# Attention in three bf16 parts instead of two float32r parts, one core

## The reference

```python
def attention(x):                       # x is layernorm(input)
    q, k, v = x @ Wq.T + bq, x @ Wk.T + bk, x @ Wv.T + bv
    q, k = rope(heads(q, 16)), rope(heads(k, 4))
    att = einsum('bhgqd,bhkd->bhgqk', q, k) / sqrt(16)
    att = softmax(where(causal, att, -inf))
    return join(einsum('bhgqk,bhkd->bhgqd', att, v)) @ Wo.T + bo

x = x + attention(layernorm(x))
h = layernorm(x)
topv, topi = top_k(h @ gate_w.T, 8);  w = softmax(topv)
x = x + sum_over_chosen(w * (silu(h @ gate) * (h @ up)) @ down) + shared(h)
```

## Time and profile before

| | us |
|---|---|
| median of 3 runs | 1209.62 (1207.33 to 1210.61) |
| the profiled execution's own time | 1211.74 |
| its span, first to last instruction | 1209.9 |

### The profile page before, as it was taken

The page is one execution under the profiler, slowest core; times in us unless marked ns, Lnnn a source line. Parts: engine busy times, 40 slices in busy tenths (PEclk is TensorE's granted clock), DMA queues, the critical chain, the costliest instruction groups (busy, mean ns, idle before and its releaser), DMA issues. The chain is left out here.

```text
span 1209.9 us, 23638 instructions
## 1 busy us (share of the span) xinstructions
PE 1031.7 (85%) x7305; PEld 812.9 (67%) x7305; DVE 705.3 (58%) x2197; ACT 662.3 (55%) x1586; POOL 717.5 (59%) x953
## 2 busy tenths in 40 slices
PE   3699888898989888989998710899989999999985
PEld 1466666666666666656665400899979999989973
DVE  2476676767676767676675370222226666666676
ACT  1466665665565656655654300566656666666651
POOL 3111122774764747747557777377777777777772
PEclk9799999999998999999998855799999999999996
DMA  2388786821321312303222794777769999998755
GB/s 94 130 258 293 237 268 208 278 101 37 108 75 57 111 44 96 114 16 101 79 95 97 275 309 164 214 217 220 219 217 335 343 337 326 366 321 305 250 196 200
DMA packets 142825, 233.20 MB, mean 193 GB/s; under 512 B 17303, under 2 KB 119910, under 8 KB 137840
## 3 DMA queue, kind: packets, MB, share of 16 engines
q1 hardware_dynamic: 67936, 101.06, 25.9%
q0 software_dynamic: 27600, 69.28, 15.9%
q10 hardware_dynamic: 47168, 61.35, 15.4%
HBM read 107.32 MB, written 132.53 MB: 198 GB/s over the span
## 5 line engine op out<-in xcount | busy, mean ns | idle before, releaser
L1495 POOL DMA_INDIRECT res_d<-y,dst_i x319 | 316.7, 993 | 114.6 <-issue 83.4
L463 POOL DMA_INDIRECT rows_d<-pay,slot_i x256 | 256.5, 1002 | 73.4 <-issue 68.4
L868 DVE TENSOR_REDUCE nmax<-ps 128x1 f32<-128x512 f32 (+3 forms) x448 | 225.7, 530 | 103.7 <-PE ps L518 101.4
L736 ACT ACTIVATE wgu_s<-ps 128x512 f32<-128x512 f32 x320 | 191.7, 600 | 95.1 <-PE ps L518 91.5
L1414 PE MATMUL psB<-wgu_s,xT 128*128 x1276 | 172.2, 279 | 4.9 <-ACT innerT L1306 4.1
L518 PE MATMUL ps<-mask,ident_b 128*128 128x256 bf16 (+1 forms) x640 | 173.3, 271 | 0.0
L511 PE MATMUL ps<-kT,qT 96*128 96x512 f32 (+3 forms) x512 | 167.4, 389 | 6.7 <-DVE nmax L868 4.2
L1431 PE MATMUL psD<-wdp_s,innerT 128*128 x638 | 166.9, 385 | 0.0
L558 PE MATMUL ps<-qT,kT 128*128 128x512 f32 (+3 forms) x512 | 162.8, 380 | 0.8 <-ACT qT L749 0.6
L1414 PEld LDWEIGHTS psB<-wgu_s,xT 128*128 128x128 f32 x1276 | 157.9, 195 | 6.1 <-issue 5.8
L1217 DVE TENSOR_TENSOR inner<-inner,psB 128x128 f32<-128x128 f32 x160 | 45.7, 286 | 194.9 <-ACT inner L1302 189.8
(11 more groups left out here) (264 smaller groups left out, 1579.5 us busy)
## 6 DMA issues: line engine op xcount, KB each, us to landing
rows_d<-blank ACTq DMA_DIRECT2D x8, 5440.0 KB, 19.5
xg<-rows_d SPq DMA_DIRECT2D x160, 272.0 KB
yk<-res_d SPq DMA_DIRECT2D x28, 1024.0 KB
wgu_s<-wgu_in ACTq DMA_DIRECT2D x8, 1024.0 KB, 14.4
x_d<-x SPq DMA_DIRECT2D x30, 192.5 KB, 2.7
xs<-x_d SPq DMA_DIRECT2D x30, 192.5 KB, 2.8
res_d<-y,dst_i POOLq DMA_INDIRECT x319
wgu_s<-x_in SPq DMA_DIRECT2D x32, 128.0 KB, 2.1
```

Source lines behind the costliest of these rows:

```text
L463: pool.indirect_dma_start(rows_d, bass.IndirectOffsetOnAxis(ap=slot_i[par][:, t, k:k + 1], axis=0), pay[par][:, t, :], None).then_inc(s_sc ...
L736: act.activation(pexp[p % 4][:, s, :], ps2[:, (5 * p + s) % 2, :], ACT.Exp, scale=HEAD_D ** -0.5).then_inc(s_exp, 1)
L868: return dve.tensor_reduce(nmax[u][:, tile, heads[0]:heads[-1] + 1], src, AX.X, ALU.max, negate=True)
L1495: pool.indirect_dma_start(res_d, bass.IndirectOffsetOnAxis(ap=dst_i[:, j % (2 * G):j % (2 * G) + 1], axis=0), y[:, j % Y, :], None, bounds ...
```

## The change

Queries, keys and maxima are split into three bf16 parts (high, middle, low). A score is one matmul over 96 rows of a single head, six products of parts: the query rows are (high, high, high, middle, middle, low) and the key rows (low, high, middle, high, middle, high), 16 rows each. Each key head is stored once instead of twice. A tile has 16 transposes for its queries and 4 for its keys, in bf16 (8 and 8 in float32r before), copied by ScalarE in two copies of 1024 columns and one of 512 (four of 512 before). The maxima have 8 transposes (4 before) and one copy of 1024 columns (512 before). VectorE splits the queries in three steps and the maxima in four operations (two before). GpSimd splits the keys, at k 8 of `pre`, in four operations; VectorE did so before. Semaphores that count these steps change with them. Ones for the maxima's rows of `kT` are filled in by VectorE once at the start instead of being part of each tile's keys. Between the phases, a wait between two VectorE steps is taken out.

```diff
-            qT = two("qT", [P, PAIRS_OF_HEADS, SEQ], F32R)
-            kT = two("kT", [P, 2 * KV_HEADS, SEQ], F32R)
+            qT = two("qT", [P, HEADS, SEQ], BF16)
+            kT = two("kT", [P, KV_HEADS, SEQ], BF16)
+            mt = two("mt", [P, 2, TILES, P], BF16)
+            qs = two("qs", [P, HEADS, 8, HEAD_D], BF16)
+            ks = two("ks", [P, KV_HEADS, 8, HEAD_D], BF16)
...
+                    if k == 8:                                   # GpSimd, pre
+                        pool.wait_ge(s_hi, tile + 1)
+                        kr = rope[u][:].rearrange("p n a d -> p (n a d)")[:, D:QK_D].rearrange("p (g d) -> p g d", d=HEAD_D)
+                        pool.tensor_tensor(kr, kr, ks[u][:, :, 1, :], ALU.subtract).then_inc(s_kstep, 1)
+                        pool.wait_ge(s_kstep, 3 * tile + 1)
+                        for part in (2, 4):
+                            last = pool.tensor_copy(ks[u][:, :, part, :], kr)
+                        last.then_inc(s_kstep, 1)
+                        pool.wait_ge(s_kstep, 3 * tile + 2)
+                        pool.tensor_tensor(ks[u][:, :, 0, :], kr, ks[u][:, :, 2, :], ALU.subtract).then_inc(s_kstep, 1)
...
+                    if k == 9:                                   # TensorE, pre
+                        pe.wait_ge(s_lo, tile + 1)
                         for half in range(2):
-                            if k == 10:
-                                pe.wait_ge(s_split, 4 * tile + half + 1)
-                            for n in range(4):
-                                last = pe.transpose(psp[:, half, n * P:(n + 1) * P].bitcast(F32R),
-                                                    src[:, 2 * half + n // 2, n % 2].rearrange("p c d -> p (c d)"), ident_r[:])
+                            for n in range(8):
+                                last = pe.transpose(psp[:, half, :].bitcast(BF16)[:, n * P:(n + 1) * P],
+                                                    qs[u][:, 8 * half + n].rearrange("p c d -> p (c d)"), ident_b[:])
                             last.then_inc(s_split_ps, 1)
+                    if k == 10:
+                        pe.wait_ge(s_kstep, 3 * (tile + 1))
+                        pe.wait_ge(s_split, 3 * tile + 1)
+                        for n in range(KV_HEADS):
+                            last = pe.transpose(psp[:, 0, :].bitcast(BF16)[:, n * P:(n + 1) * P],
+                                                ks[u][:, n].rearrange("p c d -> p (c d)"), ident_b[:])
+                        last.then_inc(s_split_ps, 1)
...
-                    pe.matmul(ps1[:, bank, at:at + keys], qT[par][0:96, p, i * P:(i + 1) * P],
-                              kT[par][0:96, 2 * (p // 2) + ab, 0:keys], start=(at == 0), stop=False,
+                    pe.matmul(ps1[:, bank, at:at + keys], qT[par][0:96, 2 * p + ab, i * P:(i + 1) * P],
+                              kT[par][0:96, p // 2, 0:keys], start=(at == 0), stop=False,
...
-                    for i in range(TILES):                       # TensorE, max_up
-                        last = pe.transpose(ps1[:, 1, i * P:(i + 1) * P].bitcast(F32R), mt[p % 2][:, i, :], ident_r[:])
+                    for n in range(2 * TILES):
+                        last = pe.transpose(ps1[:, 1, :].bitcast(BF16)[:, n * P:(n + 1) * P],
+                                            mt[p % 2][:, n // TILES, n % TILES, :], ident_b[:])
...
-                        act.copy(qs[u][:, :, 0:2, :], flat[:, 0:D].rearrange("p (n d) -> p n d", d=32).unsqueeze(2)
-                                 .to_broadcast([P, PAIRS_OF_HEADS, 2, 32]))
-                        kh = flat[:, D:QK_D].rearrange("p (g d) -> p g d", d=HEAD_D)
-                        for part in (0, 2):
-                            last = act.copy(both_places(part), kh.unsqueeze(2).to_broadcast([P, KV_HEADS, 2, HEAD_D]))
-                        last.then_inc(s_hi, 1)
+                        act.copy(qs[u][:, :, 0:3, :], flat[:, 0:D].rearrange("p (n d) -> p n d", d=HEAD_D).unsqueeze(2)
+                                 .to_broadcast([P, HEADS, 3, HEAD_D]))
+                        act.copy(ks[u][:, :, 1:6:2, :], flat[:, D:QK_D].rearrange("p (g d) -> p g d", d=HEAD_D).unsqueeze(2)
+                                 .to_broadcast([P, KV_HEADS, 3, HEAD_D])).then_inc(s_hi, 1)
...
-                        act.copy(qT[par][96:128, p, :], ps1[96:128, 1, :].bitcast(F32R)).then_inc(s_m, 1)
+                        act.copy(qT[par][96:P, 2 * p:2 * p + 2, :],
+                                 ps1[96:P, 1, :].bitcast(BF16).rearrange("p (a n) -> p a n", a=2)).then_inc(s_m, 1)
...
+                for k in range(2):                               # VectorE, at the start
+                    dve.memset(kT[k][96:P], 1.0)
...
-                        dve.tensor_tensor(qs[u][:, :, 2, :], flat[:, 0:D].rearrange("p (n d) -> p n d", d=32),
-                                          qs[u][:, :, 0, :], ALU.subtract)
-                        kf = flat[:, D:QK_D].rearrange("p (g d) -> p g d", d=HEAD_D)
-                        dve.tensor_tensor(both_places(1), kf.unsqueeze(2).to_broadcast([P, KV_HEADS, 2, HEAD_D]),
-                                          both_places(0), ALU.subtract).then_inc(s_lo, 1)
+                        qr = flat[:, 0:D].rearrange("p (n d) -> p n d", d=HEAD_D)
+                        dve.tensor_tensor(qr, qr, qs[u][:, :, 0, :], ALU.subtract).then_inc(s_qstep, 1)
+                        dve.wait_ge(s_qstep, 2 * tile + 1)
+                        dve.tensor_copy(qs[u][:, :, 3:5, :], qr.unsqueeze(2).to_broadcast([P, HEADS, 2, HEAD_D])
+                                        ).then_inc(s_qstep, 1)
+                        dve.wait_ge(s_qstep, 2 * (tile + 1))
+                        dve.tensor_tensor(qs[u][:, :, 5, :], qr, qs[u][:, :, 3, :], ALU.subtract).then_inc(s_lo, 1)
...
-                        dve.tensor_copy(mt[u][:, :, 96:98], nmax[u][:]).then_inc(s_mhi, 1)
-                        dve.wait_ge(s_mhi, U + 1)
-                        dve.tensor_tensor(mt[u][:, :, 98:100], nmax[u][:], mt[u][:, :, 96:98],
+                        largest_of = nmax[u][:].rearrange("p t a -> p a t")
+                        dve.tensor_copy(mt[u][:, :, :, 96], largest_of).then_inc(s_mhi, 1)
+                        dve.wait_ge(s_mhi, 2 * U + 1)
+                        dve.tensor_tensor(nrest[u][:], largest_of, mt[u][:, :, :, 96], ALU.subtract)
+                        dve.tensor_tensor(mt[u][:, :, :, 97], largest_of, mt[u][:, :, :, 96],
+                                          ALU.subtract).then_inc(s_mhi, 1)
+                        dve.wait_ge(s_mhi, 2 * (U + 1))
+                        dve.tensor_tensor(mt[u][:, :, :, 98], nrest[u][:], mt[u][:, :, :, 97],
                                           ALU.subtract).then_inc(s_msplit, 1)
```

More of the change, by code:

```diff
@@ L135, in build @@
             nmax = two("nmax", [P, TILES, 2], F32)
+            nrest = two("nrest", [P, 2, TILES], F32)
             oT = two("oT", [P, KV_HEADS, SEQ], F32)
@@ L172, in build @@
              s_esum, s_erec, s_rw, s_cnt_ps, s_cnt, s_new, s_base_ps, s_base, s_diag, s_rank_ps, s_thd, s_pl,
[L173 removed]
+             s_slot, s_sloti, s_tk, s_pool, s_mhi, s_var1, s_var2, s_qstep, s_kstep) = [sem(n) for n in (
                  "const_in memsets consts_converted stats1 moments1 rstd1_ready xn_ready xnT_psum xnT_ready "
@@ L180, in build @@
                  "base_ready diag_ready rank_psum rows_read place_chain slots_ready slot_ints taken_step "
-                 "pool_chain max_hi var1_ready var2_ready").split()]
+                 "pool_chain max_step var1_ready var2_ready q_split_step k_split_step").split()]
             s_late = sem("later_consts_in")
@@ L217, in ending @@
                 return isinstance(h, int) and h * 2 + par >= BATCH - n
-            def both_places(part):
-                two = ks_flat[:].rearrange("p g (a e) -> p g a e", a=2)
-                return two[:, :, :, 32 * part:32 * part + HEAD_D]
             def x2_at(h, par, t):
@@ L408, in attention_pool @@
                     pool.memset(v1[k][:, :, :, 16:17], 1.0)
-                pool.memset(row0[0:1, :], 1.0)
-                for ab in range(2):
-                    pool.memset(ks[:, :, ab, 3, ab:ab + 1].bitcast(F32), 1.0)
-                    last = pool.memset(ks[:, :, ab, 3, ab + 2:ab + 3].bitcast(F32), 1.0)
-                last.then_inc(s_memset, 1)
+                pool.memset(row0[0:1, :], 1.0).then_inc(s_memset, 1)
                 pool.wait_ge(s_const, 32)
@@ L481, in pre @@
                         pe.wait_ge(s_xn, tile + 1)
-                        pe.wait_ge(s_split, held(4 * (tile - ago + 1) - 1))
+                        pe.wait_ge(s_split, held(3 * (tile - ago + 1)))
                         for c in range(KC):
@@ L487, in pre @@
                         pe.wait_ge(s_xnT, tile + 1)
-                        pe.wait_ge(s_split, held(4 * (tile - ago + 1)))
                         for c in range(KC):
@@ L717, in pre @@
```

(22 more changed lines are left out.)

36 lines of the change are left out of this document (11 added, 25 removed).

## The result

The changed kernel took 1279.2 us (median of 4 runs, 1267.7 to 1284.2) beside 1210.1 for the kernel before (1207.3 to 1212.7): ratio 1.0554, 95% interval 1.0502 to 1.0606. I had said 1222, in a range of 1199 to 1237. The direction was right, the size was not: +67 us by the ratio (+69 by the two medians) instead of +12. The profiled execution is the quickest of the four (1267.7 us, span 1265.9), so its trace shows 56 us of it.

A forecast was written before the change was run, and what follows sets the result against it. The bound was taken to change hands between TensorE and VectorE, with GpSimd third in scatter batches. Terms summed to +13 on the profiled 1211.74, so 1225; less 2.1 for the median, 1222.6, said as 1222, range 1199 to 1237.

The forecast's parts named there:

- TensorE, scores and transposes: Attention phase: bf16 scores save 35 us, query transposes 9, maxima transposes add 6; TensorE's own time -38 us (-29 to -67).
- The weight load: TensorE's score weights: 0.20 us in f32, 0.10 in bf16; were both equal, scores save about nothing and the sum ends at 1236.
- VectorE's share: Query and maxima splits in batches 2 to 6: 5.7 us a batch added, 59% and again 60% counted, +2.0.
- The 60%: Share of TensorE's gain and VectorE's additions counted outside GpSimd's stretch, TensorE being the bound a little over half the time.
- at 60% and was hardly waited for: ScalarE's wider copies: at most +0.43 us a unit and +0.3 a tile, costed at nothing except in the first tiles.
- GpSimd, +1.8 a batch: Key split in the stretch 456 to 489 us: adds 3.0, less 1.2 us of GpSimd idling, in batches 2 to 6.
- Start, +1.5: First tiles: query split +0.85 and some 1 us of wider copies, less the shorter key part, +1.5 us.
- Batch 7, the expert phase: Last batch, with no next batch to prepare: -0.5 us; expert phase after it: unchanged.
- the forecast's sum of +13: Whole kernel: batches 2 to 6 +11, batches 0 and 1 +0.6 each, start +1.5, batch 7 -0.5.
- the marks that I named: Signs: batches 2 to 6 some 82 us, batch 1 near 76, TensorE's query wait over 20, bf16 pitch 0.28 to 0.34.
- GpSimd's gap before 475.00: GpSimd's 1.19 us wait in a scatter batch; forecast gone, with VectorE's wait for `rstd` grown to about 2 us.
- Rival 3: VectorE and GpSimd operations collide in the same slots: 19 us, 60% felt, +11, 1234 us (to 1245); chance 0.14.

The follow-up runs named there:

- the test: Kernel before with the maxima's split at the changed kernel's four operations, remainder and third part into spare places: 1224.6 us, ratio 1.0120.
- all four costs off: Changed kernel without GpSimd's key parts, with one query subtraction, two maxima operations and ScalarE's copies as fp32 words: 1189.8 us, ratio 0.9870.

## Why the prediction was wrong in size

By its own steps:

- *TensorE, scores and transposes* (-38 us of its time, of which -14 entered the sum: -1.7 in five batches and 60% of 4.7 in two). The pitches are 0.28 and 0.33, as forecast, except behind fp32 matmuls, where I had not looked and where 0.02 a group is saved. The 14 to 16 us measured agree with the 14, but they hold the shorter key steps of VectorE and ScalarE too, so that the agreement may be luck: the share of its own time that TensorE passes on stays open.
- *The weight load.* A bf16 load of the scores took 101 ns (L560, 472 loads, 43.6 us) where the earlier trace rows have 202 in f32. The Trainium skill (TensorE: Matmul & The Clock Gate, section LDWEIGHTS) works it out from the columns alone, which makes it one duration for both; the traces disagree with it, and the end of 1236 that followed from it had no ground, though it lay nearer to the result.
- **VectorE's share, "5.7 a batch (8 x 0.3 + 4 x 0.85), by 59% and again 60%": the step that failed.** Queries and maxima were put at 46 us of work, and 17 of them went into the sum (+2.0 in five batches, 60% of 5.7 in two). Added alone to the kernel before, they cost 29 + 15 = 44, for 28 + 17 = 45 us of longer steps, nearly all of them where 35% was charged. The prices were right, within 4 us each; the discount was not. The 60% stood for TensorE being "the bound there a little more than half of the time", with no row behind it, and it was taken for TensorE and VectorE alike. Yet I had written that the query split "stands right before the transposes for which TensorE already waits", and the earlier trace rows had that wait in 9 tiles. For a step that is waited for like this, nearly the whole of its growth counted.
- *ScalarE, "at 60% and was hardly waited for, so I cost it at nothing but in the first tiles"*: failed by 20 us in the changed kernel (7 for the maxima copy in the kernel before). The earlier trace rows had ScalarE idle 25.7 us before that copy, waiting for the maxima's transposes. An engine that idles until its input comes, and whose output is what the next pass starts with, can be a link of the chain at any share.
- *GpSimd, +1.8 a batch*: the operations took 1.26 us a tile in three dependent steps, 1.34 from the first to the next scatter (511.09 to 512.43), inside my bounds of 1.2 to 2.0. The queue's part, 13 us, is near the 9 that I summed. The other 15 are the wait for a key part that stands behind scatters. I had counted what is queued behind the new operations, and not what is queued ahead of them. In the five batches they cost 5.0 each when added alone (75.1 to 82.3 us became 80.4 to 88.0).
- *Start, +1.5*: the first mark came 15.4 us late, of which the first scores account for 4.1 (49.58 to 53.73 us); the rest are batches 0 and 1 at some 5.6 each, which I had at 0.6. GpSimd has no scatters there, and the key operations alone moved this mark by 3.2 us (214.4), the query operations by 10.0 (221.1), the maxima's by 4.6: it is VectorE's part above all.
- *Batch 7, the expert phase*: near. Between the last two marks it is +0.9 us, forecast -0.5; the expert phase, forecast unchanged, is 2.4 shorter.

Of the 54 us between the forecast's sum of +13 and the 67, VectorE's two terms make 27, GpSimd's 19 and ScalarE's 11, the last with the tiles' copies; TensorE's 2 and the start's 1.5, which lies in these terms, go the other way.

The books balance: 29 + 15 + 28 + 7, measured by addition to the kernel before, 4 for the tiles' copies (20 less 16), less the 16 of TensorE's side, is 67, and 67 was measured. The sum mixes both kernels, and its terms are good to 3 to 6 us each, some 11 together, and it lacks the 6 us by which the changed kernel's maxima take longer than those of the test. So it closes to the microsecond by luck; the 4 alone could be nothing.

Of the marks that I named: batches 2 to 6 did not grow by 2 us but, mark to mark, by 8.1, 6.4, 11.3, 9.1 and 6.9; batch 1 was not within 1 us (some 5.6, above); TensorE's wait for the queries came to 18.1, not over 20; VectorE's longest wait for `rstd` is 2.3 (forecast 2); the bf16 pitch is as forecast, and so, within 3 us, is the expert phase. GpSimd's gap before 475.00 should have gone. At the same place of a batch in the changed kernel there is

```profile
520.12 0.23 POOL L447 TENSOR_SCALAR rstd<-mv 128x1 f32<-128x1 f32 x1 [1.14 <-DVE mv L925]
```

24.1 us behind its mark (496.07) instead of 20.1 (475.00 behind 454.95). GpSimd still idles there: in this stretch, in which the forecast saw GpSimd alone, the other engines' additions counted as well. Rival 3, collisions of VectorE and GpSimd, had the direction of the miss and not its cause: VectorE's query operations kept their 0.44 us on average.

One part stays open. TensorE's mean granted clock in the batches between marks was 0.93 to 0.98 before, with TensorE busy 89 to 92% of them, and 0.89 to 0.96 in the changed kernel, at 78 to 83%; with all four costs off it was 0.98 to 0.99, at 85 to 89% (2.4 GHz is 1.00, 1.2 GHz 0.50). So a part of the 67 us may be clock: with 3% less of it, TensorE's 72 us of a batch are some 2 us longer, if all of them count (an estimate). What the clock follows here no run tells apart: the version with one maximum and copies as words had 0.97 to 1.00 at 80 to 84% busy, much the share of the changed kernel.

## What to carry to other kernels

When no engine is above 90% and each waits for another in turn, don't discount an added operation by busy shares: look for who waits for its result, and how often. In the kernel before, an addition to the queries' split, awaited in every tile, cost all of its time (29 us for 28), and one to the maxima, awaited in every unit, nearly all (15 for 17). One to ScalarE's copy cost 7 for 26, GpSimd's key operations 28 for 40 awaited and 13 for 40 not awaited. So "in full" is the upper bound to start from, and a discount needs a place in the timeline that shows it. For a step moved to a busy queue ask two questions, what stands behind it and what stands ahead of it. When one engine's part gets shorter, expect the wait to pass to the next. And before splitting a value in three parts, ask whether it needs more than one.

## What the hardware showed that I had not expected

- ScalarE's copy from PSUM takes its time by elements, not by bytes: 1024 bf16 elements 1.00 us, the same bits as 512 fp32 words 0.578. The rewrite gave 1.7% of the whole.
- A bf16 score behind four fp32 matmuls of 193 columns starts 0.76 us after the first of them, an f32r score 0.59 after it; that takes back nearly the whole gain of the group behind (medians over 28 places, matmul to mask: 0.38 after 0.40).
- GpSimd's operations of 64 elements took 0.28 to 0.36 us, against 0.54 for 160 and 0.74 for 256 in the earlier trace rows: by these rows some 0.2 us of each doesn't depend on size (an estimate), so that small operations there are dear in number.
